# Batch 0 of the strided convolution writes straight into the array that the clustering reads

## What is computed

```python
# layer 0: sx is (8, 512, 128, 128); w_down (256, 2, 3, 3)
x = conv_general_dilated(sx, w_down, window_strides=(2, 2), padding=((1, 1), (1, 1)),
                         feature_group_count=256)          # -> (8, 256, 64, 64)
xx = x[0].reshape(256, 64 * 64)                            # batch 0 alone
xs = (xx - min over row) / (max over row - min over row)
labels = kmeans of the 256 rows of xs, 8 clusters, 10 rounds
soh = one-hot of the labels, sorted by the spread of each cluster's mean of xx
v5 = per batch, mean of x over the channels of each cluster   # (8, 8, 4096)
mu, var = two-component Gaussian mixture per batch, 10 rounds
gate = sigmoid(...)[:, label]
out = bilinear upsampling by 2 of (gate * x + x) * w_up, plus sx
# layer 1: + bias, FIR upsampling by 2, leaky ReLU, FIR downsampling by 2
```

## Time and profile before

| | |
|---|---|
| time, median of 3 runs | 7528.47 us |
| lowest and highest of them | 7528.38 and 7532.02 us |
| time of the profiled execution | 7524.66 us |
| its span, first to last instruction | 7522.9 us |
| TensorE busy | 7038.6 us, 94% of the span |
| VectorE busy | 5921.7 us, 79% |
| ScalarE busy | 4569.9 us, 61% |
| GpSimd busy | 2523.5 us, 34% |
| mean granted TensorE clock | 0.968 of full speed |

### The profile page before, as it was taken

How to read it: one execution, slowest core, us unless ns; L and a number is a source line. 1 busy time by engine, 2 the same in 40 slices (tenths; PEclk the granted TensorE clock), 3 DMA queues, 4 the chain that set the end, 5 groups by cost and what they waited for, 6 DMA issues and landing times.

```text
span 7522.9 us, 691936 instructions
## 1 busy us (share of the span) xinstructions
PE 7038.6 (94%) x302277; PEld 6399.7 (85%) x302277; DVE 5921.7 (79%) x11620; ACT 4569.9 (61%) x9038; POOL 2523.5 (34%) x3076
## 2 busy tenths in 40 slices
PE   6699993089999999999999999999999999999999
PEld 2444441079999999999999999999999999999998
DVE  7399998967777777777777777777777777777776
ACT  0100002357777777777777777777777777777776
POOL 0000000034444444444444444444444444444443
PEclk9799996589999999999999999999999999999999
DMA  6188883023333333333333333333333333333332
GB/s 259 59 321 316 324 316 111 0 78 95 97 96 95 98 95 96 96 95 97 96 95 98 95 96 97 95 96 96 95 97 95 96 97 95 97 96 95 97 95 82
DMA packets 1261249, 891.87 MB, mean 119 GB/s; under 512 B 184336, under 2 KB 1234960, under 8 KB 1244432
## 3 DMA queue, kind: packets, MB, share of 16 engines
q1 hardware_dynamic: 1249936, 856.58, 36.9%
q10 hardware_dynamic: 11264, 34.61, 1.6%
HBM read 587.94 MB, written 303.04 MB: 118 GB/s over the span
## 4 chain that ended last, share of the span: by engine, by line
PE 79%; issue 0%; DVE 0%; DMA 0%; ACT 0%; SPq 0%; POOL 0%; DVEq 0%
PE bank L1087 26%; PE bank L1082 25%; PE twin L1082 13%; PE twin L1087 13%; PE twin L1217 2%; DVE x_sum L1315 0%; DMA img<-in_x 0%; DVE leaky L1291 0%; DMA low<-conv_dram 0%; SPq L993 0%; POOL img L1041 0%; SPq L994 0%; DVE up L1300 0%; ACT dn L1282 0%; ACT res L1267 0%
## 5 line engine op out<-in xcount | busy, mean ns | idle before, releaser
L1291 DVE SCALAR_TENSOR_TENSOR leaky<-bank,slope_t 128x512 f32<-128x512 f32 x4096 | 2634.4, 684 | 1036.8 <-ACT slope_t L1251 1036.8
L1082 PE MATMUL bank<-up_t,up 64*64 64x133 f32 x65536 | 2761.8, 276 | 2.0 <-issue 1.2
L1087 PEld LDWEIGHTS bank<-down_t,leaky 64*64 64x64 f32 x131072 | 2241.0, 135 | 101.5 <-issue 92.6
L1087 PE MATMUL bank<-down_t,leaky 64*64 64x35 f32 (+1 forms) x131072 | 2312.1, 222 | 13.5 <-issue 11.6
L1251 ACT ACTIVATE slope_t<-bank 128x512 f32<-128x512 f32 x4096 | 2226.2, 600 | 2.7 <-PE bank L1082 2.7
L1082 PEld LDWEIGHTS bank<-up_t,up 64*64 64x64 f32 x65536 | 2044.6, 134 | 3.3 <-issue 3.3
L1050 POOL TENSOR_TENSOR low_d<-low_v 128x252 f32<-128x252 f32 x512 | 311.2, 608 | 4901.9 <-ACT low_v L1273 4901.9
L1267 ACT ACTIVATE res<-twin 128x512 f32<-128x512 f32 x1024 | 611.5, 597 | 1452.9 <-PE twin L1087 1452.9
L1315 DVE SCALAR_TENSOR_TENSOR x_sum<-lift,coef,img 128x128 f32<-128x128 f32 x4096 | 1432.5, 409 | 11.8 <-POOL img L1041 11.8
L1082 PE MATMUL twin<-up_t,x_sum 64*64 64x133 f32 x32768 | 1385.9, 278 | 7.5 <-DVE x_sum L1315 5.3
L1087 PE MATMUL twin<-down_t,dn 64*64 64x35 f32 (+1 forms) x65536 | 1359.7, 222 | 7.1 <-issue 6.7
(11 more groups left out here) (159 smaller groups left out, 1788.0 us busy)
## 6 DMA issues: line engine op xcount, KB each, us to landing
img<-in_x SPq DMA_DIRECT2D x1024, 256.0 KB, 2.9
out<-res SPq DMA_DIRECT2D x1024, 256.0 KB, 2.4
rows_next<-in_x SPq DMA_DIRECT2D x42, 4224.0 KB, 13.9
rows_next<-in_x SPq DMA_DIRECT2D x14, 4096.0 KB, 13.5
low<-conv_dram SPq DMA_DIRECT2D x1024, 32.0 KB, 2.2
conv_dram<-conv_next ACTq DMA_DIRECT2D x56, 512.0 KB, 4.1
rows_in<-in_x SPq DMA_DIRECT2D x6, 4224.0 KB, 14.0
rows_in<-in_x SPq DMA_DIRECT2D x2, 4096.0 KB, 29.1
```

The lines of the kernel that those rows point to most:

```text
L1082: return pe.matmul(acc[cols(c), a:b], src[cols(rt), cols(c)], up_t[cols(rt), a:b], start=first, stop=False, skip_group_check=True)
L1087: return pe.matmul(acc[cols(c), a:b], src[cols(rt)], down_t[cols(rt), k, a:b], start=first, stop=False, skip_group_check=True)
L1291: v.scalar_tensor_tensor(out=leaky[1 - m % 2][:, e, i].rearrange("p k w -> p (k w)"), in0=u2_acc[e][i][:], scalar=GAIN, in1=slope_t[e][i][ ...
```

## The change

The convolution of batch 0 writes its tiles into `xx`. Tile n is the band `n // CB` of channel block `n % CB`, which is 1024 elements in a row in each partition, as the buffers `conv` were. `xx` is now allocated ahead of `first_convolution`, behind the same three arrays as before, and the other arrays of `first_convolution` stand behind it. The two `conv` buffers go, and with them the waits for their stores. The stores to `conv_dram` stay, since `resample` reads them, and ScalarE still waits for all of them at the end of the block. The loads back, their semaphore and the wait for them go, so that SyncE has nothing to do in `clusters`.

```diff
-        def first_convolution():
+        def first_convolution(xx):
...
-                conv = [sb(f"conv{i}", [P, QR, WO]) for i in range(2)]
+                tiles = [xx[:, n % CB, n // CB * QR * WO:(n // CB + 1) * QR * WO].rearrange("p (r w) -> p r w", r=QR) for n in range(UB)]
                 in_loaded = [sem(f"in_loaded{i}") for i in range(2)]
-                conv_stored = [sem(f"conv_stored{i}") for i in range(2)]
+                conv_stored = sem("conv_stored")
...
                         v.wait_ge(in_loaded[n % 2], 16 * (n // 2 + 1))
-                        if n >= 2:
-                            v.wait_ge(conv_stored[n % 2], 16 * (n // 2))
                         for s, (i, kh, kw) in enumerate(order):
                             r0 = 1 if (q == 0 and kh == 0) else 0
-                            dst = conv[n % 2][:, r0:V_ROWS, (1 if kw == 0 else 0):]
+                            dst = tiles[n][:, r0:V_ROWS, (1 if kw == 0 else 0):]
...
                         act.wait_ge(t_done, n + 1)
-                        if n >= 2:
-                            act.wait_ge(conv_stored[n % 2], 16 * (n // 2))
-                        nc.scalar.activation(conv[n % 2][:, V_ROWS:, :].rearrange("p r w -> p (r w)"),
+                        nc.scalar.activation(tiles[n][:, V_ROWS:, :].rearrange("p r w -> p (r w)"),
                                              bank[n % 2][:, 0:T_ROWS * WO], ACT.Copy).then_inc(t_copied, 1)
                         act.wait_ge(t_copied, n + 1)
                         act.wait_ge(v_done, n + 1)
                         act.dma_start(conv_dram[cb * P:(cb + 1) * P, q * QR * WO:(q + 1) * QR * WO],
-                                      conv[n % 2][:].rearrange("p r w -> p (r w)")).then_inc(conv_stored[n % 2], 16)
-                    for i in range(2):
-                        act.wait_ge(conv_stored[i], 16 * UB // 2)
+                                      tiles[n].rearrange("p r w -> p (r w)")).then_inc(conv_stored, 16)
+                    act.wait_ge(conv_stored, 16 * UB)
...
-                @block.sync
-                def _(sp):
-                    for cb in range(CB):
-                        sp.dma_start(xx[:, cb, :], conv_dram[cb * P:(cb + 1) * P]).then_inc(xx_loaded, 16)
-
...
                     v.wait_ge(padded, 1)
-                    v.wait_ge(xx_loaded, 16 * CB)
                     v.tensor_reduce(mn[:], xx[:], AX.X, ALU.min).then_inc(step, 1)
...
-            first_convolution()
             xx = own.enter_context(nc.sbuf_tensor("xx", [P, CB, PX], F32))
+            first_convolution(xx)
```

More of the change, by code:

```diff
@@ L460, in clusters @@
                 padded = sem("padded")
-                xx_loaded = sem("xx_loaded")
                 step = sem("step")
```

## The result

The changed kernel takes 7518.07 us in the median of 20 runs (7515.64 to 7522.07), the kernel before 7530.86 us (7528.20 to 7535.18, 20 runs). The ratio is 0.9983 with a 95% interval of 0.9976 to 0.9990, so it is faster by 0.17%, or 12.8 us, with an interval from 0.10 to 0.24%. The forecast was 0.165% less, 7516.0 us, against a median of 7528.47 at that time. The profiled execution took 7515.76 us with a span of 7514.0, which is 8.9 us less than the span of the profiled execution before.

A forecast was written before the change was run, and what follows sets the result against it. TensorE in `resample` fills 79% of the span, but the exposed wait for the `xx` loads was priced: 12.45 us off the 7528.47 us median, all other terms at 0, gives 7516.0 us, range 7511.4 to 7523.3.

The forecast's parts named there:

- The reload: Before VectorE's row minimum in clustering: dropping both loads of `xx` and their wait starts it at 162.80, not 175.25, gaining 12.45 us.
- What stays: Between the last store's issue and the clustering: the 3.1 us up to SyncE going on are kept, including 2.7 us of landing.
- The waits for the buffers: In the first convolution: VectorE's six waits for `conv` buffers, taken as 0, with bounds of 0 and 0.13 us gained.
- the taps in `xx`: In the first convolution: 144 tap operations, 8 copies and 8 stores keep their shapes at a new address; cost taken as 0.
- The clock: TensorE's clock changes from the transposes to the cluster means: taken as 0, bounds 1.5 us gained to 3.8 lost.
- the clock's bounds ahead of the Gram matrix: At the transposes: a rise delay of 4.6 us may become 2.7 or 6.9, so 0.95 us gained to 1.15 lost.
- The last block: The block reading `conv_dram`: only its start moves and its length stays, 5972.9 us, expected as 5973.
- A gain past 0.2%: Rival for the whole kernel: waits and clock add 2.6 us to the gain, passing 15.06 us; chance 12%.
- The dearer taps: Rival in the first convolution: taps in `xx` cost 10% more, 11.8 us in all, leaving 7527.8 us; chance 4%.
- the clock that stays low through the Gram matrix: Rival at the 128 Gram matmuls: at 1.2 GHz throughout they take 27.9 us more, giving 7543.9 us; chance 3%.

## Why the prediction was right

**The reload (12.45 us).** Right in place, mechanism and size. In three traces of each kernel the minimum moved from 12.62 to 0.15 us after the memset, 12.47 us, and putting the loads back alone undid the change. That the chain of waits had it at 0% of the span didn't matter: it was on the path, with nothing beside it. That the medians differ by 12.8 us, within 0.4 of the forecast, is partly luck: the interval of the ratio goes from 7.5 to 18 us. The size rests on the traces.

By the fixed cost and rate that the Trainium skill gives for the software path ("DMA: Bandwidth & Descriptors", "Anatomy of one DMA — SWDGE (gpsimd) path"), one load would take an estimated 6.8 us and both 11.6. These loads went through a hardware queue of SyncE, and measured from the memset to the minimum they added 7.9 us for one and 12.5 to 13.1 for both. So the rate was near it (402 to 456 GB/s against 436), and the fixed part here larger, by 0.6 to 1.3 us over its 2.0.

**What stays.** Right: the store's issue to the memset is 3.2 us as before. Of it 2.35 us go from the chain when the store is awaited later.

**The waits for the buffers, and the taps in `xx`.** Both taken at 0, and both right as far as can be told: the taps take 819 and 817 ns, and with the loads back and everything else changed the ratio is 1.0001, give or take 0.1%.

**The clock (taken at 0, bounds 1.5 gained to 3.8 lost).** Within the bounds. In the first pair of traces the cluster means lost 1.5 us and the transposes regained 0.3. Over three traces of each kernel, the next block starts 179.65 - 167.69 = 11.95 us sooner from the last store, so the clock took 0.5 us of the 12.47 on average. Nothing here ties that to the change, and nothing rules it out. One of the expected values was summed wrongly: the clock's bounds ahead of the Gram matrix, 0.95 gained to 1.15 lost, give a gain of 11.3 to 13.4 us at its start and not 11.7 to 13.6. Measured it is 208.11 - 195.75 = 12.36, inside both. I had expected the next block's load near 326.0; it came at 327.6, by these 1.5 us and the 0.4 by which the last store was late, less the 0.3.

**The last block.** The expected 5973 us was no length of the block: the window of the earlier trace rows begins at 1550, and the block's first upsampling matmul is at 1532.89. That its length stays was also too firm, for it differs by 2.8 us between the three executions of the kernel before alone. From the first upsampling matmul to the last copy it took 5986.6 to 5989.4 us in the kernel before and 5988.8 to 5990.7 in the changed one. The spreads overlap, and the difference of the means, 1.4 us, can't be told from their spread. In the seven other kernels, which all have the tiles in `xx`, one trace each gives 5985.4 to 5992.8 us, on both sides of the kernel before. Nothing in the change reaches this block, but the experiments don't settle whether it is one us longer.

**The rivals.** A gain past 0.2% didn't come: 12.8 us where 15.1 were needed, though the interval goes up to 0.24%. The dearer taps and the clock that stays low through the Gram matrix can both be ruled out here: 817 ns, and a rise at 189.8, before the first Gram matmul at 195.75.

## What to carry to other kernels

A wait that is two thousandths of the span can be priced to well under 1 us if it stands between two meetings of all engines and no engine has work beside it: take the idle time in brackets, and check what the first instruction behind it can start on. The bytes matter then, not only the trip: without half of the reload 4.6 to 5.2 us of 12.5 to 13.1 came back, and only no reload gave back the rest. When gains of one or two us are at stake, compare the same stretch in several traces of each kernel; two traces each that agree can still mislead, as the cluster means showed.

## What the runs showed of the hardware that was not expected

The same 32 matmuls of the cluster means took 15.25, 15.35 and 16.70 us in one and the same kernel, by a clock that rose from 1.2 to 2.4 GHz 2.7, 3.0 or 5.7 us after the dense work began. In all thirteen traces here the length was either 15.2 to 15.5 or 16.6 to 16.8 us, and none lay between. In one trace, work pushed back by 1.8 us reached the next block only 0.8 us later. The Trainium skill ("TensorE: Matmul & The Clock Gate", Part 1) says that the count of matmuls at the low clock differs from run to run of one kernel; the three traces of the kernel before agree.
